# A graph layer on one core: h in two fp16 parts instead of three bf16 parts

## The reference, cut to what matters

```python
# x (6250, 64) f32; src, dst (206250,) int32, dst sorted; edge (206250, 64) f32
h = maximum(layernorm(x), 0)
msg = h[src] + edge
agg = segment_sum(msg, dst, 6250)
out = x + relu(agg @ W1 + b1) @ W2 + b2
```

## Time and profile before

| | |
|---|---|
| median of 3 runs | 515.69 us (514.45 to 516.74) |
| the profiled execution | 520.9 us, span 519.1 us |
| busy in the span | PE 462.3 us, DVE 435.6, ACT 385.4, POOL 330.1 |
| granted TensorE clock, mean | 0.996 |

### The profile page before, as it was taken

How to read it: one execution, slowest core, us unless ns; L and a number is a source line. 1 busy time by engine, 2 the same in 40 slices (tenths; PEclk the granted TensorE clock), 3 DMA queues, 4 the chain that set the end, 5 groups by cost and what they waited for, 6 DMA issues and landing times.

```text
span 519.1 us, 28271 instructions
## 1 busy us (share of the span) xinstructions
PE 462.3 (89%) x12541; PEld 406.7 (78%) x12541; DVE 435.6 (84%) x536; ACT 385.4 (74%) x525; POOL 330.1 (64%) x226
## 2 busy tenths in 40 slices
PE   1014799899999999999999999999999999999994
PEld 1003689788888888888888888888898888888884
DVE  4789998977988898898898889889888988969550
ACT  2679778677787788787878778878787877877720
POOL 5587995655596677668668766866966875215100
PEclk9999999999999999999999999999999999999998
DMA  9677038744645555555564565556555456554300
GB/s 204 193 210 201 11 110 219 200 125 123 185 123 151 158 140 137 148 168 139 130 180 131 145 156 154 142 131 180 131 151 156 137 141 157 144 144 112 98 3 10
DMA packets 142767, 73.70 MB, mean 142 GB/s; under 512 B 26780, under 2 KB 140686, under 8 KB 142518
## 3 DMA queue, kind: packets, MB, share of 16 engines
q1 hardware_dynamic: 139241, 65.32, 47.1%
q0 software_dynamic: 3168, 4.90, 4.0%
q10 hardware_dynamic: 234, 1.65, 0.8%
HBM read 66.98 MB, written 4.86 MB: 138 GB/s over the span
## 4 chain that ended last, share of the span: by engine, by line
PE 88%; DVE 5%; DMA 2%; ACT 2%; issue 2%; POOL 0%; SPq 0%; DVEq 0%
PE sum_ps L889 27%; PE sum_ps L911 21%; PE count_ps L876 18%; PE sum_ps L897 14%; PE sum_ps L926 3%; PE sum_ps L933 3%; ACT h_sb L381 2%; PE sum_ps L861 1%; DMA g<-in_dst,row_i 1%; DMA dst_sb<-in_dst 1%; DVE counts L638 1%; DVE var L614 1%; DVE counts L675 1%; DVE h_parts L679 1%; DVE hi_hot L713 1%
## 5 line engine op out<-in xcount | busy, mean ns | idle before, releaser
L433 ACT CAST counts<-count_ps 128x882 bf16<-128x882 f32 (+2 forms) x369 | 327.1, 973 | 58.4 <-PE count_ps L876 56.7
L713 DVE TENSOR_TENSOR lo_hot<-lo_table,codes 128x3328 bf16<-128x3328 bf16 (+3 forms) x123 | 232.6, 1891 | 44.7 <-PE count_ps L876 41.6
L540 POOL DMA_INDIRECT ell<-comb_rows,ell_idx x50 | 123.5, 2470 | 99.1 <-DVE ell_idx L685 70.4
L889 PE MATMUL sum_ps<-counts,h_parts 128*128 128x256 bf16 (+1 forms) x1225 | 145.6, 273 | 0.0
L876 PE MATMUL count_ps<-hi_hot,lo_hot 64*128 64x49 bf16 x6256 | 115.2, 183 | 22.0 <-DVE hi_hot L713 11.4
L876 PEld LDWEIGHTS count_ps<-hi_hot,lo_hot 64*128 64x128 bf16 x6256 | 98.0, 94 | 44.8 <-issue 29.0
L889 PEld LDWEIGHTS sum_ps<-counts,h_parts 128*128 128x128 bf16 x1225 | 114.4, 99 | 18.5 <-issue 0.3
L911 PE MATMUL sum_ps<-e_hot,edges 128*64 128x24 f32 x3528 | 112.3, 217 | 0.2 <-issue 0.2
L911 PEld LDWEIGHTS sum_ps<-e_hot,edges 128*64 128x64 f32 x3528 | 107.0, 138 | 3.0 <-issue 0.4
L520 POOL DMA_INDIRECT g<-in_dst,row_i x49 | 89.1, 1818 | 21.2 <-issue 11.1
L713 DVE TENSOR_TENSOR hi_hot<-hi_table,codes 128x1300 bf16<-128x1300 bf16 (+3 forms) x123 | 102.6, 834 | 0.0
(11 more groups left out here) (111 smaller groups left out, 200.8 us busy)
## 6 DMA issues: line engine op xcount, KB each, us to landing
edges<-in_edge_attr SPq DMA_DIRECT2D x294, 192.0 KB
h_rows<-h_sb SPq DMA_DIRECT2D x1, 1568.0 KB, 10.2
x_sb<-in_x SPq DMA_DIRECT2D x4, 384.0 KB, 10.0
out<-o_sb SPq DMA_DIRECT2D x24, 64.0 KB
comb_rows<-counts ACTq DMA_DIRECT2D x1, 1443.8 KB
dst_rows<-in_dst SPq DMA_DIRECT2D x49, 18.0 KB
ell<-comb_rows,ell_idx POOLq DMA_INDIRECT x50
g<-in_dst,row_i POOLq DMA_INDIRECT x49
```

The source lines that it names most:

```text
L433: nc.scalar.copy(counts[j % 2][:, :, 0:2 * half].rearrange("p s (h i) -> p h s i", h=2)[:, :, :, first + a:first + b], count_ps[u % 3][:, ...
L540: nc.gpsimd.indirect_dma_start(out=ell[j % 2][0:rows, h, :, :].rearrange("p s w -> p (s w)"), out_offset=None, in_=comb_dram[:, :], in_off ...
L713: return nc.vector.tensor_tensor(out_ap.rearrange("p i (a t) -> p i a t", t=2), bc(table_ap.rearrange("p (o a t) -> p o a t", o=1, t=2), [ ...
L889: nc.tensor.matmul(sum_ps[m % 2][:, 0:cols], parts[:, s, 0:2 * F], counts[m % 2][:, s, 0:cols], start=(s == 0), stop=False, skip_group_che ...
```

## The change

h is scaled by 8192 and split into two fp16 parts: ScalarE makes the first, VectorE the remainder h x 8192 minus the first part. The counts are stored as fp16 times 1/8192, so the product needs no further scale. Both parts together are the 128 columns of one matmul per node tile, and low_sums is gone. rest_of_h moves behind batch 2 of period 0 and rest_of_rest is gone. The small reduction nobody reads now follows three batches in every period (0, 2 and 3; in period 0, 1, 3 and 4).

```diff
+    H_SCALE = 8192.0
...
-        h_parts = sb("h_parts", [P, NT, 3, F], bf16)
-        counts = [sb(f"counts{b}", [P, NT, 2 * P], bf16) for b in range(2)]
+        h_parts = sb("h_parts", [P, NT, 2, F], f16)
+        counts = [sb(f"counts{b}", [P, NT, 2 * P], f16) for b in range(2)]
...
-                def take_part(part):
-                    if part == 0:
-                        act.wait_ge(h_made, SLICES - ACT_SLICES)
-                        act.wait_ge(h_scaled, ACT_SLICES)
-                        nc.scalar.copy(h_parts[:, :, 0, :], tops(h_sb)).then_inc(part_made, 1)
-                    else:
-                        act.wait_ge(rest_made, 1)
-                        nc.scalar.copy(h_parts[:, :, 1, :], tops(rest_sb)).then_inc(part_made, 1)
+                def take_part():
+                    act.wait_ge(h_made, SLICES - ACT_SLICES)
+                    act.wait_ge(h_scaled, ACT_SLICES)
+                    nc.scalar.activation(h_parts[:, :, 0, :], h_sb[:, :, :], ACT.Copy, scale=H_SCALE).then_inc(part_made, 1)
...
-                    nc.scalar.copy(
+                    nc.scalar.activation(
                         counts[j % 2][:, :, 0:2 * half].rearrange("p s (h i) -> p h s i", h=2)[:, :, :, first + a:first + b],
-                        count_ps[u % 3][:, :, 0:(b - a) * NT].rearrange("p h (i s) -> p h s i", s=NT)).then_inc(copied, 1)
+                        count_ps[u % 3][:, :, 0:(b - a) * NT].rearrange("p h (i s) -> p h s i", s=NT),
+                        ACT.Copy, scale=1.0 / H_SCALE).then_inc(copied, 1)
...
-                    if j == 1:
-                        act.wait_ge(rest_in_parts, 1)
...
                         if j == 0 and u == 2:
-                            take_part(0)
-                        if j == 0 and u == 5:
-                            take_part(1)
+                            take_part()
...
                 def rest_of_h():
-                    dve.wait_ge(h_made, SLICES - ACT_SLICES)
-                    dve.wait_ge(h_scaled, ACT_SLICES)
-                    nc.vector.tensor_tensor(rest_sb, h_sb[:, :, :], tops(h_sb), ALU.subtract).then_inc(rest_made, 1)
-
-                def rest_of_rest():
-                    dve.wait_ge(rest_made, 1)
-                    nc.vector.tensor_tensor(h_parts[:, :, 2, :], rest_sb, tops(rest_sb), ALU.subtract
-                                            ).then_inc(rest_in_parts, 1)
+                    dve.wait_ge(part_made, 1)
+                    nc.vector.scalar_tensor_tensor(out=h_parts[:, :, 1, :], in0=h_sb[:, :, :], scalar=H_SCALE,
+                                                   in1=h_parts[:, :, 0, :], op0=ALU.mult, op1=ALU.subtract
+                                                   ).then_inc(rest_in_parts, 1)
...
-                        if j < 3 and b in ((1, 3, 4), (0, 2, 3), (0, 2, 3))[j]:
+                        if b in ((1, 3, 4) if j == 0 else (0, 2, 3)):
                             one_input(batch_index(j, b))
-                        if j == 0 and b == 1:
+                        if j == 0 and b == 2:
                             rest_of_h()
-                        if j == 0 and b == 3:
-                            rest_of_rest()
...
-                def high_sums(m, his):
+                def node_sums(m, his):
                     cols = sum_cols(m)
+                    last = None
                     for s in his:
-                        nc.tensor.matmul(sum_ps[m % 2][:, 0:cols], parts[:, s, 0:2 * F],
-                                         counts[m % 2][:, s, 0:cols], start=(s == 0), stop=False,
-                                         skip_group_check=True)
-
-                def low_sums(m, his):
-                    cols = sum_cols(m)
-                    for s in his:
-                        half = slice(s % 2 * F, s % 2 * F + F)
-                        last = nc.tensor.matmul(sum_ps[m % 2][half, 0:cols], parts[:, s, 2 * F:3 * F],
-                                                counts[m % 2][:, s, 0:cols], start=False, stop=False,
+                        last = nc.tensor.matmul(sum_ps[m % 2][:, 0:cols], parts[:, s, :],
+                                                counts[m % 2][:, s, 0:cols], start=(s == 0), stop=False,
                                                 skip_group_check=True)
                     return last
...
-                HIGH = [0, 20, 20, 40, 40, 49]
-                LOW = [0, 0, 5, 5, 17, 49]
-                assert HIGH[-1] == NT and LOW[-1] == NT
+                NODES = [0, 17, 17, 33, 33, 49]
+                assert NODES[-1] == NT
```

More of the change, by code:

```diff
@@ L7, in build_gnn_layer @@
 def build_gnn_layer(nc, x, src, dst, edge, w1, b1, w2, b2, out):
-    f32, i32, bf16 = mybir.dt.float32, mybir.dt.int32, mybir.dt.bfloat16
+    f32, i32, bf16, f16 = mybir.dt.float32, mybir.dt.int32, mybir.dt.bfloat16, mybir.dt.float16
     ALU = mybir.AluOpType
@@ L47, in build_gnn_layer @@
     LO_STEP = 1 << LO_SHIFT
+    H_SCALE = 8192.0
+    assert F - 1 < 8 * 8
     BATCHES = [[26, 26, 26, 25, 25], [19, 19, 18]]
@@ L103, in build_gnn_layer @@
         h_sb = sb("h_sb", [P, NT, F])
-        h_parts = sb("h_parts", [P, NT, 3, F], bf16)
-        counts = [sb(f"counts{b}", [P, NT, 2 * P], bf16) for b in range(2)]
-        arena = [counts[b][:, :, :].rearrange("p s q -> p (s q)") for b in range(2)]
+        h_parts = sb("h_parts", [P, NT, 2, F], f16)
+        counts = [sb(f"counts{b}", [P, NT, 2 * P], f16) for b in range(2)]
+        arena = [counts[b][:, :, :].rearrange("p s q -> p (s q)").bitcast(bf16) for b in range(2)]
         edges = [sb(f"edges{b}", [P, CK, KK * F]) for b in range(SLOT_EDGES)]
@@ L124, in build_gnn_layer @@
         comb_nodes = comb_sb.bitcast(f32).rearrange("p (e q) -> p e q", q=2)[:, :, 1]
-        rest_sb = sq_sb
-        def tops(ap):
-            return ap[:, :, :].rearrange("p t f -> p (t f)").bitcast(bf16).rearrange("p (t f q) -> p t f q", t=NT, q=2)[:, :, :, 1]
         out_of_order = h_sb[0:ROWP, :, :].rearrange("p t f -> p (t f)")[:, 0:PER]
@@ L168, in build_gnn_layer @@
         ident_b = sb("ident_b", [P, P], bf16)
-        unread = sb("unread", [P, 3 * ROUNDS])
+        unread = sb("unread", [P, ROUNDS * DTS])
         mean = sb("mean", [P, NT])
@@ L233, in build_gnn_layer @@
             sem("mean_made"), sem("mean_sub"), sem("squared"), sem("var_made"), sem("std_made"), sem("scale_made"))
-        h_made, h_scaled, h_out, part_made, rest_made = (
-            sem("h_made"), sem("h_scaled"), sem("h_out"), sem("part_made"), sem("rest_made"))
+        h_made, h_scaled, h_out, part_made = (
+            sem("h_made"), sem("h_scaled"), sem("h_out"), sem("part_made"))
         rest_in_parts = sem("rest_in_parts")
@@ L959, in _ @@
                                 if m == 0:
-                                    pe.wait_ge(part_made, 2)
+                                    pe.wait_ge(part_made, 1)
                                     pe.wait_ge(rest_in_parts, 1)
@@ L967, in _ @@
                                     pe.wait_ge(far_read, 1)
-                            high_sums(m, range(HIGH[v], HIGH[v + 1]))
+                            last = node_sums(m, range(NODES[v], NODES[v + 1]))
                             if v % 2 == 1 and v // 2 < tiles_in(m):
                                 edge_sums(m, v // 2, range(TILES_E))
-                            if LOW[v] < LOW[v + 1]:
-                                last = low_sums(m, range(LOW[v], LOW[v + 1]))
                             if v == ROUNDS - 1:
```

## The result

The changed kernel takes 474.36 us (median of 4 runs, 472.1 to 478.54), the kernel before 516.22 beside it: ratio 0.920, 95% interval 0.913 to 0.928. Forecast were 468 us and a range of 457 to 485. The profiled execution took 478.54 us with a span of 476.7, the longest of its four runs, at a mean granted clock of 0.978.

A forecast was written before the change was run, and what follows sets the result against it. TensorE was taken as the wall at 18.48 us a period, then VectorE at 16.7. Start 1.2 + middle 42.7 + tail 4.1 = 48.0 off 520.9 gives 472.9, times 0.990 is 468 us; range 457 to 485.

The forecast's parts named there:

- likeliest case: VectorE becomes the wall at 16.3 to 17.0 us a period, 459 to 475 us in all; chance 0.62.
- The start: Period 0: one subtraction of 3.33 us goes, VectorE waits 3.4 for part_made; net 1.2 us gained, first TensorE period at 55.1.
- The middle: Periods 1 to 23 at 16.7 us plus two small terms: 387.1 us instead of 429.8, a gain of 42.7.
- the 16.03: VectorE's period in us without waits or GpSimd's disturbance, three small sums included; 0.7 for GpSimd makes it 16.7.
- the stop of 2.26: VectorE's one long stop that has nothing to do with TensorE, added once to the middle as 2.26 us.
- the wait for the shift: VectorE's wait on the shift at j = 22, estimated at 0.7 us and added to the middle.
- rival (a): ScalarE becomes the wall through dearer count copies: 17.4 us a period, 484 us; chance 0.12.
- rival (b): GpSimd takes more of VectorE's time: 17.0 to 17.6 us a period, 475 to 489 us; chance 0.17.
- (c): GpSimd starves beside a never idle VectorE; match and edge loads wait, 615 us at rounds of 23.1 us; chance 0.03.
- the round of 13.3 us: Earlier trace's GpSimd round, 68.68 to 82.02, with VectorE as full; taken as evidence against GpSimd starving.
- the round of 23.1 us: Earlier trace's GpSimd round, 45.54 to 68.68, with VectorE never idle; the ground for the rival that GpSimd starves.
- The tail: The 32.94 us from 486.16, TensorE's, lose low sums of 2.87 and 1.3 us: a gain of 4.1.

The follow-up runs named there:

- thin edges: The changed kernel with edge loads bringing a third of the rows from period 2 on, older rows staying; 469.74 us, ratio 0.910 to the kernel before.
- half the edge_hots: The changed kernel with edge_hots making only half of its one-hot table from m = 1 on, the rest stale; 478.23 us, ratio 0.892.
- before + sums: The kernel before with the small sums in every period, one part of the change alone; 520.81 us, ratio 0.997.
- bias on TensorE: The changed kernel with b2 added by TensorE matmuls instead of by GpSimd's add_bias; 501.89 us, ratio 0.965.
- rest behind batch 3: The changed kernel with rest_of_h behind batch 3 of period 0 instead of batch 2; 496.18 us, ratio 0.941.

## Why the prediction was right

The time lies in the range and 6.4 us above the forecast, whose likeliest case (16.3 to 17.0 a period) happened. Term by term, in the profiled execution (476.7 against a forecast span of 471.1):

**The start.** VectorE stands still for part_made, as forecast 3.4 us, and the new subtraction takes the 3.43 of the old. VectorE's and ScalarE's timelines, against the earlier trace rows:

```profile
44.37 3.43 DVE L665 SCALAR_TENSOR_TENSOR h_parts<-h_sb,h_parts 128x3136 f16<-128x3136 f32 x1 [3.47 <-ACT h_parts L386]
47.71 0.47 DVE L686 SCALAR_TENSOR_TENSOR hi_m<-ell,node_f 128x64 bf16<-128x64 f32 x2
```

```profile
41.52 2.82 ACT L386 ACTIVATE h_parts<-h_sb 128x3136 f16<-128x3136 f32 x1
```

The whole part was 0.87 later than in the execution before (ScalarE's copy at 41.52, not 40.65), so TensorE's first period starts at 56.01 instead of 55.1; less that shift the gain is the 1.2 of the forecast.

**The middle.** Periods 1 to 23 take 390.6 us (56.01 to 446.65), forecast 387.1. The mechanism stands: VectorE is the wall, at 16.59 a period without the two long ones. That the size agrees is in part luck. VectorE's own steady pace with three sums is 16.46 (65.86/4 with thin edges, VectorE busy for 65.72 of it), and 16.34 without sums. So the sums cost 0.12 a period and not 0.27, and GpSimd's disturbance over the 16.03 is 0.4 and not 0.7. What the forecast did not have made up for it: the two long periods, together 8.3 us over 16.59, and shorter delays by late instructions and slots. Of the two small terms, the stop of 2.26 did not come back (VectorE has no stop between 83.77 and 86.23, where batch 4 of period 2 runs), and the wait for the shift was 2.4, not 0.7.

**ScalarE.** The count copy as an activation, against the earlier trace rows:

```profile
L427 ACT ACTIVATE counts<-count_ps 128x882 f16<-128x882 f32 x192 | 189.9, 1034 | 41.2 <-PE count_ps L861 38.2 <-issue 2.6
```

13 ns more than the CAST, forecast 18; rival (a) falls. Its pace matters in one place that I had not seen, TensorE's stop of 0.50.

**TensorE** needs 16.04, not 15.61. The node sums and the missing low sums cost what was forecast (15.54 busy; the 0.67 of the prediction's second low-sum group is 0.66 in the earlier trace rows); the term left out was that stop. It was harmless, for VectorE's pace is above it, but the slack left is some 0.5 us and not 1.1, and TensorE is not seen waiting for hi_hot in the quiet periods.

**GpSimd** is the step that was wrong: I forecast rounds of 13 to 15 us, never waited for. Its 20 rounds from 68.34 to 402.48 take 16.71 each, just VectorE's period, its gathers take up to 4.98 us, and it was waited for 4 times. In kind this is rival (b) and a little of (c), by a price of a few us. The forecast rested on the round of 13.3 us, which had small sums; but the round of 23.1 us had them too, five between 45.54 and 68.68, so their presence is not what tells the two apart.

What a gather waits for shows in its length. Between 60 and 440 us of the fourteen traces, the 40 gathers of slots during which VectorE stands still for at least 80% of the time take 0.94 to 0.96 us; the 380 during which it is idle for less than 2% take 3.1 on average and up to 9.59. The 16 of the changed kernel that take over 3.2 us all end 0.78 to 0.90 us after VectorE has begun an operation with a single input, a small sum or the reduction in count_below, and the nine of over 9 us in the two traces without the sums end 0.78 or 0.79 after that reduction. The Trainium skill ("SBUF — State Buffer", SBUF: two separate sides) lets a VectorE operation with two SBUF inputs and a GpSimd operation that reads SBUF exclude each other from a shared port pair, each for its whole length. The trace agrees if a gather, whose indices lie in SBUF, is such a reader: a pair takes 9.45 us beside VectorE's tables and 1.88 where VectorE stands still (263.86 and 265.11 us with half the edge_hots). Not every gather has to wait for a single-input operation, though: many end in 1.4 to 2.6 us without one, and rounds keep pace with VectorE even without the added sums.

**The tail** took 30.05 us, forecast 28.84. The matmuls saved are there (454 for 551), but at a lower clock, 0.88 instead of 0.94: besides the stretch at the very end that both executions have, the clock falls once more (0.57 from 459.00 to 463.00). That this makes the 1.2 us is not shown.

## What to carry to other kernels

When the last slack of the bounding engine is taken away, forecast the pace of every engine including its fixed stops, and then add a term for stretches in which all are within half a us of each other: here 8 us of 391, and more in kernels that differ by one moved instruction. Before judging such a kernel by a second version of it, look at the periods one by one; runs of one kernel differed by up to 8% (462.2 to 497.8), and kernels with the same quiet periods by 2 to 3%, on different chips. A forecast by the next tighter wall was good to 1.4% here, and edits that save less than that could not be argued from busy times. And before an operation that does no work is thrown out, look at what its neighbours get done beside it: without the small sums VectorE's period is 0.12 us shorter and GpSimd's longest gather twice as long.

## What the runs showed of the hardware

- **The clock can fall behind short stops.** One stop of 1.50 us (with one of 0.42 before it), two of 0.63 and 0.78, and one of 2.16 were followed by 6.8, 6.8 and 10.2 us at the lower level (0.50 granted, 16 sums in 3.28 to 3.59 us instead of 1.92). Those three periods were 4.8, 3.5 and 6.4 us over a quiet one, 2.5 to 3 times the stops (the first holds the stop of 1.05 too, which came under the lower clock). The length of a stop does not decide it alone: single stops of 0.87 and 1.06 (186.86 and 323.07 in the changed kernel) had no fall behind them, a stop of about 1.45 at the same place had one in before + sums (92.70) and none in the kernel before (92.67), and with the bias on TensorE the clock fell at 172.4 though the last stop, of 0.45, had ended at 163.58. With 16 node sums fewer a period the mean clock was 0.915, and the kernel no faster.
- **GpSimd's gathers go by what VectorE runs beside them**: 0.94 us where it stands still, up to 3.08, 4.99 and 9.59 us beside back-to-back tables with five, three and no small sums a period.
- **TensorE's instructions can come late**, several times at the same places of the program in several kernels, by 0.3 to 2.0 us; 9 times over 0.4 us with full edge loads and 3 with thin ones on the same chip. On the first two chips they also came late as a series of 0.51 us gaps, mostly with 3 to 6 matmuls between. Chips and edits were not crossed, so which of them makes the series is open.
- **Whole kernels settle into rhythms**: 16.04, 16.34, 16.46, 16.92 and 17.0 us held over many periods, one kernel against another; the 16.92 of rest behind batch 3 comes from an edit that touches period 0 alone.
